# Single-head attention computed with the sources on the partitions, and the adjacency mask also stored turned

## The reference

```python
def gat_conv(x, src, dst, W, a_src, a_dst, b):
    h = x @ W
    s = h @ a_src
    d = h @ a_dst
    alpha = jax.nn.leaky_relu(s[src] + d[dst], 0.2)
    m = jax.ops.segment_max(alpha, dst, num_segments=n)
    ex = jnp.exp(alpha - m[dst])
    denom = jax.ops.segment_sum(ex, dst, num_segments=n)
    w = ex / (denom[dst] + 1e-16)
    return jax.ops.segment_sum(h[src] * w[:, None], dst, num_segments=n) + b
```

## Time and profile before

| | us |
|---|---|
| median of 3 runs (lowest, highest) | 4386.68 (4383.18, 4397.35) |
| the profiled execution's own time | 4381.9 |
| its span, first to last instruction | 4380.3 |

### The profile page before, as it was taken

The page is one execution under the profiler, slowest core; times in us unless marked ns, Lnnn a source line. Parts: engine busy times, 40 slices in busy tenths (PEclk is TensorE's granted clock), DMA queues, the critical chain, the costliest instruction groups (busy, mean ns, idle before and its releaser), DMA issues. The chain is left out here.

```text
span 4380.3 us, 72251 instructions
## 1 busy us (share of the span) xinstructions
PE 3495.6 (80%) x25428; PEld 2519.0 (58%) x25429; DVE 3066.7 (70%) x4546; ACT 2200.6 (50%) x3295; POOL 215.8 (5%) x212
## 2 busy tenths in 40 slices
PE   3555554688888868888883799949996999799799
PEld 1222223466666646666662466548885888688677
DVE  6888986799999879999985222255544554555456
ACT  2444441788888868888880111114442444244322
POOL 0000000000000000000000244400000000000010
PEclk8656666899999989999995899969998999899889
DMA  1111112311111031111103722233313330333220
GB/s 44 62 63 70 61 64 55 120 64 62 58 53 63 33 121 62 62 63 47 63 33 122 252 46 46 41 124 120 114 57 122 117 117 30 136 117 117 73 66 30
DMA packets 135678, 347.31 MB, mean 79 GB/s; under 512 B 28337, under 2 KB 106423, under 8 KB 117847
## 3 DMA queue, kind: packets, MB, share of 16 engines
q1 hardware_dynamic: 114240, 313.75, 20.3%
q0 software_dynamic: 13888, 20.07, 2.5%
q10 hardware_dynamic: 7254, 9.67, 0.6%
HBM read 278.31 MB, written 65.14 MB: 78 GB/s over the span
## 5 line engine op out<-in xcount | busy, mean ns | idle before, releaser
L817 ACT ACTIVATE a_probsT<-a_psT 128x896 f32<-128x896 f32 (+1 forms) x1100 | 900.6, 836 | 765.5 <-PE a_psT L938 763.1
L938 PE MATMUL a_psT<-ident,a_scores 128*128 128x128 f32 (+1 forms) x6875 | 1009.3, 286 | 134.0 <-ACT a_scores L809 117.5
L859 DVE SCALAR_TENSOR_TENSOR a_scores<-a_el,hx 128x3136 f32<-128x3136 f32 x275 | 956.7, 3479 | 91.9 <-DMA a_mask<-mask_dram 65.4
L938 PEld LDWEIGHTS a_psT<-ident,a_scores 128*128 128x128 f32 (+1 forms) x6875 | 770.5, 143 | 336.9 <-issue 193.5
L863 DVE CUSTOM_DVE_ANT_0 a_scores<-a_scores,a_mask 128x3136 f32<-128x3136 f32 x275 | 940.5, 3420 | 11.8
L809 ACT ACTIVATE a_scores<-a_scores,a_negmax 128x1664 f32<-128x1664 f32 (+1 forms) x550 | 879.1, 1598 | 43.7 <-DVE a_negmax L863 43.7
L957 PE MATMUL a_psO<-hx,a_probsT 128*128 128x256 f32 (+1 forms) x3750 | 874.8, 381 | 0.0
L957 PEld LDWEIGHTS a_psO<-hx,a_probsT 128*128 128x128 f32 (+1 forms) x3750 | 680.2, 189 | 107.3 <-issue 25.7
L954 PE MATMUL a_psO<-a_probsT,hx 128*32 128x128 f32 (+1 forms) x10000 | 586.3, 287 | 118.9 <-ACT a_probsT L817 116.1
L356 PE MATMUL cnt<-onehot_c,onehot_dst_a 128*128 128x392 bf16 x1200 | 363.9, 463 | 305.5 <-DVE onehot_c L294 256.4
L954 PEld LDWEIGHTS a_psO<-a_probsT,hx 128*32 128x32 f32 (+1 forms) x10000 | 324.2, 110 | 319.9 <-ACT a_probsT L817 171.6
(11 more groups left out here) (239 smaller groups left out, 2484.8 us busy)
## 6 DMA issues: line engine op xcount, KB each, us to landing
a_mask<-mask_dram SPq DMA_DIRECT2D x125, 1568.0 KB, 6.7
mask_dram<-logc SPq DMA_DIRECT2D x200, 196.0 KB, 1.9
moe_w<-in_L_ffn_w SPq DMA_DIRECT2D x48, 512.0 KB
a_el<-el_dram ACTq DMA_DIRECT2D x6, 1568.0 KB, 15.5
a_el<-el_dram SPq DMA_DIRECT2D x5, 1568.0 KB, 6.5
x<-n_x SPq DMA_DIRECT2D x2, 3072.0 KB
n_x<-in_x SPq DMA_DIRECT2D x8, 640.0 KB, 7.3
n_x<-x SPq DMA_DIRECT2D x8, 640.0 KB, 6.3
```

Source lines behind the costliest of these rows:

```text
L817: nc.scalar.activation(pT[:, gi % 2, 0:w], psT[gi % 2][:, 0:w], ACT.Copy).then_inc(s_ev, 1)
L859: nc.vector.scalar_tensor_tensor(sc[:, c, :], el[:, k % H, 0, :], col(hx, b + k // H, D + h0 + k % H), el[:, k % H, 1, :], ALU.subtract, A ...
L938: last = nc.tensor.transpose(psT[gi % 2][0:r, t * P:(t + 1) * P], sc[:, k % 3, c0:c0 + r], g["ident"][:, :])
```

## The change

- The adjacency phase also makes maskT_dram, the same matrix with the sources as rows. When the eight windows of a block of destinations are stored, SyncE loads the block back (`load_rows`), TensorE turns it in five chunks of five 128x128 tiles (`transposes`), one chunk behind each of the last five windows of the next eight, ScalarE copies each chunk out of PSUM (`copy_T`), and SyncE stores it (`store_T`). The loops of ScalarE and SyncE are written out; TensorE's loop is arranged anew.
- The single-head layers call a new function, `gat_phase`. It goes over nine panels of destinations (one of 128, then eight of 384); within a panel, over the 25 blocks of sources a, which lie on the partitions. `lowest` keeps the running minimum over the sources of the mask plus the source term, for the next panel; TensorE turns that one tile, VectorE reduces it, works out two numbers per destination, and TensorE and ScalarE spread them over the partitions (`spread`). `leaky` and `masked` make the scores of one source block; ScalarE takes the exponential; the result is already the stationary operand of the product. A column of ones beside the 256 features gives the sum of the probabilities.
- Self loops are also written to the diagonal of maskT_dram, for the first 1250 nodes; keeping and restoring the old diagonal is gone.

The core of the diff (the rest is declarations and loop bookkeeping):

```diff
 # adjacency_phase, TensorE, behind the matmuls of window n*RUN+j
+                    q = chunk(n * RUN + j)
+                    if q is not None:
+                        transposes(i, q)
+            def transposes(i, q):
+                if q % TPC == 0:
+                    pe.wait_ge(s_rows, i * (16 * RPB) + (16 * (q // TPC + 1)))
+                if q >= 2:
+                    pe.wait_ge(s_mTc, i * (RPB * TPC) + (q - 1))
+                for t in range(TPW):
...
+                    last = nc.tensor.transpose(psM[q % 2][0:r, t * P:(t + 1) * P], rowsB[:, q // TPC % 2, c0:c0 + r],
+                                               g["ident"][:, :])
+        def chunk(w):
+            b, j = w // WPB - 1, w % WPB - (WPB - TPC)
+            return b * TPC + j if b >= 0 and j >= 0 else None
 # ScalarE
+            def copy_T(q):
+                act.wait_ge(s_mT, q + 1)
+                if q >= 2:
+                    act.wait_ge(s_mTo[q % 2], stored(q - 2))
...
+            for w in range(WIN):
+                act.wait_ge(s_used, w + 3)
...
+                if w + AHEAD < WIN:
+                    stage(0, w + AHEAD, w + AHEAD >= SS)
+                if w and chunk(w - 1) is not None:
+                    copy_T(chunk(w - 1))
 # SyncE
+            for w in range(WIN):
+                sp.wait_ge(s_mask, w + 1)
+                sp.dma_start(view[w:w + 1, :, :].rearrange("o p c -> (o p) c"), logc[:, w % ROWS, :]).then_inc(s_out[w % ROWS], 16)
+                if w >= WPB and w % WPB == 0:
+                    load_rows(w // WPB - 1)
+                if w >= 2 and chunk(w - 2) is not None:
+                    store_T(chunk(w - 2))
+            load_rows(NB - 1)
+            for q in range((NB - 1) * TPC - 2, NB * TPC):
+                store_T(q)
 # node_phase
-                act.dma_start(g["diag_dram"].rearrange("(r q) -> r q", q=LOOP_Q), lv[:, 0, :]).then_inc(s_lout, 16)
+                act.dma_start(diagonal(g["maskT_dram"], R1, LOOP_Q), loop(3)[0:R1], allow_slow_non_contiguous=True).then_inc(s_lout, 16)
 # gat_phase (new), VectorE
+            def lowest(n, a):
...
+                    dve.wait_ge(s_low, n * NB + a)
+                    nc.vector.scalar_tensor_tensor(low[0:r, n % 2, 0:w], mk[0:r, n % 2, a, 0:w], nel[0:r, a:a + 1],
+                                                   low[0:r, n % 2, 0:w], ALU.add, ALU.min).then_inc(s_low, 1)
+            def leaky(n, a):
...
+                if u >= 3:
+                    dve.wait_ge(s_p, u - 2)
+                nc.vector.scalar_tensor_tensor(z[0:r, u % 3, 0:w], ab[0:r, n % 2, 0, 0:w], nel8[0:r, a:a + 1],
+                                               ab[0:r, n % 2, 1, 0:w], ALU.add, ALU.min).then_inc(s_branch, 1)
+            def masked(n, a):
...
+                dve.wait_ge(s_branch, u + 1)
+                nc.vector.tensor_tensor(z[0:r, u % 3, 0:w], z[0:r, u % 3, 0:w], mk[0:r, n % 2, a, 0:w], ALU.add).then_inc(s_z, 1)
+            for n in range(L):
+                more = n + 1 < L
+                for a in range(NB):
+                    if more and a <= 12:
+                        lowest(n + 1, 2 * a)
+                    leaky(n, a)
+                    if more and a < 12:
+                        lowest(n + 1, 2 * a + 1)
+                    masked(n, a)
+                    if n:
+                        if a == 8:
+                            denominators(n - 1)
+                        elif a == 9:
+                            reciprocals(n - 1)
+                        elif 10 <= a < 10 + PANELS[n - 1][1]:
+                            outputs(n - 1, a - 10)
+                    if more and 16 <= a < 20:
+                        (reduce_low, top_z, top, branches)[a - 16](n + 1)
 # gat_phase, ScalarE and TensorE, for each source block
+                    nc.scalar.activation(pr[0:r, u % 4, 0:w], z[0:r, u % 3, 0:w], ACT.Exp, scale=-1.0,
+                                         bias=eb[0:r, a:a + 1]).then_inc(s_p, 1)
...
+                    for j in range(k):
+                        last = nc.tensor.matmul(bank(n, j)[:, 0:D + 1], pr[0:r, u % 4, j * P:(j + 1) * P], hx[0:r, a, 0:D + 1],
+                                                start=a == 0, stop=a == NB - 1)
+                    if n + 1 < L and a == 14:
+                        turn(n + 1)
+                    if n + 1 < L and a == 20:
+                        spread(n + 1)
 # program
-                attention_phase(nc, g, f"a{l}", hx, y, 1, 0, 1, 3, bias=a[f"L1_gnn_b{l}"])
+                gat_phase(nc, g, f"a{l}", hx, y, a[f"L1_gnn_b{l}"])
```

More of the change, by code:

```diff
@@ L358, in windows, with run @@
                     last.then_inc(s_used, 1)
-            pe.wait_ge(s_k, 4)
-            blocks(pe, windows)
+                    q = chunk(n * RUN + j)
+                    if q is not None:
+                        transposes(i, q)
+            def run(i, n):
+                most = load(pe, 3, i * 2 + n, ET)
+                with pe.If(most > 0):
+                    windows(i, n, True)
+                with pe.If(most < 1):
+                    windows(i, n, False)
+            pe.wait_ge(s_k, 4)
+            run(0, 0)
+            with pe.Fori(0, RUNS // 2) as i:
+                run(i, 1)
+                run(i, 2)
+            for q in range((NB - 1) * TPC, NB * TPC):
+                transposes(0, q)
         @block.gpsimd
@@ L382, in stage @@
                 nc.scalar.activation(stC[:, j % SS, :], g["codes"][:, 1, bass.ds(lo, GROUP)], ACT.Copy).then_inc(s_st, 1)
[L384 to L393, removed]
+            def copy_T(q):
+                act.wait_ge(s_mT, q + 1)
+                if q >= 2:
+                    act.wait_ge(s_mTo[q % 2], stored(q - 2))
+                r = P if q % TPC < TPC - 1 else NS - (TPC * TPW - 1) * P
+                full = TPW * P if r == P else (TPW - 1) * P
+                last = nc.scalar.activation(rowsT[:, q % 2, 0:full], psM[q % 2][:, 0:full], ACT.Copy)
+                if r < P:
+                    last = nc.scalar.activation(rowsT[0:r, q % 2, full:full + P], psM[q % 2][0:r, full:full + P], ACT.Copy)
+                last.then_inc(s_mTc, 1)
@@ L401, in _, with load_rows, store_T @@
+            for q in range((NB - 1) * TPC - 1, NB * TPC):
+                copy_T(q)
         @block.sync
         def _(sp):
+            def load_rows(b):
+                for j in range(WPB):
+                    sp.wait_ge(s_out[(b * WPB + j) % ROWS], (b * WPB + j) // ROWS * 16 + 32)
+                if b >= 2:
+                    sp.wait_ge(s_mT, (b - 1) * TPC)
+                sp.dma_start(rowsB[:, b % 2, :], g["mask_dram"][b * P:(b + 1) * P, :]).then_inc(s_rows, 16)
+            def store_T(q):
+                sp.wait_ge(s_mTc, q + 1)
+                a0, b = q % TPC * TPW, q // TPC
+                out = g["maskT_dram"][a0 * P:(a0 + TPW) * P, b * P:(b + 1) * P].rearrange("(t p) c -> p t c", p=P)
+                tiles = rowsT[:, q % 2, :].rearrange("p (t c) -> p t c", c=P)
+                if q % TPC < TPC - 1:
+                    sp.dma_start(out, tiles).then_inc(s_mTo[q % 2], 16)
+                else:
+                    r = NS - (TPC * TPW - 1) * P
+                    sp.dma_start(out[:, 0:TPW - 1, :], tiles[:, 0:TPW - 1, :]).then_inc(s_mTo[q % 2], 16)
+                    sp.dma_start(out[0:r, TPW - 1, :], tiles[0:r, TPW - 1, :]).then_inc(s_mTo[q % 2], 16)
@@ L415 @@
+            load_rows(NB - 1)
+            for q in range((NB - 1) * TPC - 2, NB * TPC):
+                store_T(q)
+            for i in range(2):
+                sp.wait_ge(s_mTo[i], stored(NB * TPC - 1 - i))
 FULL = N // P
@@ L429, with diagonal @@
 L1_LOOPS = 1250
[L432 to L436, removed]
+def diagonal(rows_, rows, cols):
+    flat = rows_.rearrange("a b -> (a b)")
+    step = rows_.shape[1] + 1
+    return flat[0:rows * cols * step].rearrange("(r q s) -> r q s", q=cols, s=step)[:, :, 0:1]
 LOOP_Q = 25
@@ L441 @@
 assert LOOP_R * LOOP_Q == N and LOOP_R <= P
[L442 to L444 removed]
+assert L1_LOOPS % LOOP_Q == 0
 PART = 5
```

213 lines of the change are left out of this document (188 added, 25 removed).

## The result

The changed kernel takes 4596.68 us (median; 4591.08 to 4599.93) against 4386.35 (4383.18 to 4397.35) in runs on the same chip: a ratio of 1.0473, interval [1.0452, 1.0495]. It is slower by 210 us, where the forecast said 179 (4565). The direction and the two places are as forecast; two sizes are off by about a third, one cost was set at nothing, and the errors partly cancel. The profiled execution's span is 4593.1 us, 212.8 more than before.

The account below looks back on a forecast made before the run. TensorE was taken to bound the layers and VectorE, nearly, the counting; after the change VectorE bounds the layers. 4381.9 + 51 (layers) + 130 (counting) = 4563, stated as 4565 us on the median's scale, range 4460 to 4690.

Parts of the forecast that it names:

- The layers, +17 each: Single-head layers: 387 us against 370.4 with VectorE as the bound, +51 us for three.
- Unit 2.09: Layers, source blocks 0 to 11: VectorE's four instructions take 2.09 us, against 1.29 on TensorE.
- The dependent pair: Layers, from block 13 on: VectorE's second instruction waits for the first's end, 0.13 us lost, 1.14 us a pair.
- The half-rate rule: Layers: a skill rule that would cost `leaky` and `lowest` 0.4 us more each, some 160 us a layer; not adopted.
- Counting, between the windows +110: Edge counting: waits for stores and row loads cost about 4.5 us a block, x 24 = 110 us.
- The ring: Counting: combine, store, copy, small operands, next one-hots form a cycle of 7.7 us for two windows, against 6.03 or 5.48.
- The tail, +20: End of counting: nothing hides the last block's store, load, turning and stores; 22 us against 1.9 before, +20.
- The first node phase, 0: Diagonal's edits cost 0: one small DMA issue takes another's place on ScalarE.
- Counting hides its additions: Rival for counting: only the tail and 1 to 2 us a block stay, +55; 4490 us in all; chance 0.17.
- TensorE-bound layers: Rival for the layers: VectorE's unit falls below TensorE's 1.29 us, a layer is 305 us, total 4317; chance 0.05.
- Clock falls in the layers: Rival for the layers: TensorE's idle gaps lower its clock, about +48 us a layer, total 4705; chance 0.13.
- Landings of 4 us or more: Rival for counting: slow store landings, three rounds a block at 9.4 us, +190 to 200 there, total 4630; chance 0.12.

Follow-up runs that it names:

- e5_few_minima: Changed kernel with most of `lowest` left out in the layers (only every fifth source block from panel 1 on): 4394.1 us.
- e2: Changed kernel with five buffers of copied, turned rows in place of two, so the copy waits for a store of the block before: 4528.2 us.
- e4: Changed kernel with both counting edits, five buffers of turned rows and the turning begun two windows later: 4423.6 us.
- e14: Kernel e3 with the turned chunk's store issued ahead of the next block's row load on SyncE instead of right behind it: 4572.0 us.
- e10: Kernel before the change plus 5 unread transposes of the identity behind five windows of every eight in counting: 4362.4 us, ratio 0.9936.
- after: The changed kernel itself, as measured against the kernel before: 4596.7 us, ratio 1.0473.
- e3: Changed kernel with the turning of a block begun two windows later, two buffers kept: 4615.8 us.
- e13: Changed kernel with both counting edits, diagonal stores on SyncE, and `lowest` replaced by an upper bound worked out once a layer: 4176.2 us.
- e6: Changed kernel with `masked` moved from VectorE to GpSimd, five score buffers, and `lowest` spread over 15 source blocks: 4690.7 us.

## Why the prediction was right, and where its sizes were off

**What bounds what.** Right. VectorE took TensorE's place in the layers, and e5_few_minima shows it: less work on VectorE alone, and a layer falls to 315.6 us, with TensorE not idle in the 250 us shown. Of the signs that were named, VectorE was 93% busy in the layer (forecast 95%), TensorE 84% (75%), ScalarE's wait for the store came 65 times in 24 blocks at 2.4 us (three times a block at 3), and the counting took 799 us instead of 760.

**The total.** Closer than its terms: the layers were put 14 us too high in all and the counting 39 too low, and these errors partly cancel. That is luck.

**The layers, +17 each: measured +12.3.** Start 18.8, measured 18.4. Unit 2.09, measured 2.06. Panel 43.4, measured 42.6 (the step that makes the denominators, 3204.18 in one panel and 3246.80 in the next); seven panels of 0.8 less, and the shorter start, cover the 4.3 us by which the layer of 387 was too long. The dependent pair was 1.12, forecast 1.14. The half-rate rule that was weighed there (the Trainium skill, Vector Engine (DVE) Microarchitecture Reference, Points that are easy to get wrong: scalar_tensor_tensor with two non-bf16 SBUF inputs) did not hold: 0.61 us for 384 columns. By the prediction's working a layer would have been over 500 us with it.

**Counting, between the windows +110: measured +149.4**, 6.2 us a block instead of 4.5. The ring was the right one: the rows above show it, and it is gone in e2 and e4. Three things were mis-sized. The row load lands in 7.5 us, not 6.7; why is not shown. TensorE's wait for the copy two chunks back (77.7 us, 33 times) was not named: with it the products of the next window stand behind a copy that stands behind a store. And the waits were costed one by one and added, 3.3 to 4.4 for the store and 1.1 for the load; taken away, they give 2.6 us a block and minus 0.8 (plus 1.0 with the stores in the order of e14), and together 7.1. So neither is a term of its own: with one gone, the other takes much of the time that it leaves, as TensorE's wait for the row load did in e2 (64.4 to 110.3 us).

**The clock in counting** was taken as it stood, 0.64. With the transposes and without the waits it is 0.83, and e10 puts 22 us on that. Against e4, which does the same work without the waits, after is 170 us longer up to the last combine, not 149. No term and no rival had this gain; the rival on the clock looked only for a loss, and in the layers, where the clock was 0.95 (0.63 from 3110 to 3147, 1.00 after that).

**The tail, +20: measured +18.5.** Right.

**The first node phase, 0: measured +4.4.** The step said that one small DMA issue takes another's place on ScalarE. The one that went took 0.34 us, the one that came 5.66, for 1250 elements that lie one row and one column apart, and the square root is behind it. It starts 27.4 us after the phase's start, before 23.7, which is 3.7 of the 4.4 us.

**The rivals.** Counting hides its additions: out (168 us). TensorE-bound layers: out, until `lowest` is gone; then the layer is 303 to 316 us, where that rival had 305. Clock falls in the layers: out. Landings of 4 us or more: the median was 2.5, but in e3 a copy went on only 8 us after its store was issued behind the row load, and there the whole counting, with its tail, is 191 us longer than before, where the rival had 190 to 200.

## What to carry to other kernels

Before a second consumer is put on in-order queues in a tight loop, list what stands behind each of its waits, and give it so many buffers that the longest landing is over before a buffer comes round again. Two waits that each look small are to be taken away together before they are judged. Ask which store stands right behind a large load in the queue, and who waits for it: here the copy behind such a store went on 8 us after the store's issue, where the median landing was 2.5, and putting the store ahead of the load gave 44 us back. When an instruction stream is moved off a bound engine, count the passes that the new layout adds on the next one: here 625 transposes went and a third pass on VectorE came, and only without that pass and without the waits in the counting (e13) was the new layout faster than the old one.

## What the runs showed of the hardware that was not expected

- With f32 transposes between the products of the counting TensorE's granted clock was 0.83, without them 0.64; 625 unused ones made the kernel before 0.64% faster (e10).
- VectorE's scalar_tensor_tensor of 384 columns took up to 1.35 us instead of 0.61 while GpSimd's tensor_tensor ran (e6).
- A store of 320 KB issued 0.39 us behind a load of 1568 KB let the copy that waited for it go on after 8.0 us (e3); the median landing of such stores in after was 2.5.
- The issue of a DMA of 1250 single elements into a diagonal of a matrix with rows of 3200 elements took 5.66 us of its engine's queue, and that of 3125 elements into one with rows of 3136 took 0.86. What makes the difference is not shown.
